# A four-layer network on one core: layer 0's gathers tied to its chain, layer 1's two branches in one stage, layer 3's attention written out

## The chip, the cores and the metric

The kernel runs on one core of one Trainium2 chip. The time is device microseconds of that core for one execution, and the median of the runs counts. Besides them one execution was recorded by the hardware profiler.

## What is computed

`x` is one sequence of 2048 tokens of 128 features, in float32. Each of four layers adds two branches that read the same normalised input; shortened from the reference:

```
xn = layernorm(x)
x = x + L0_attn(xn) + L0_ffn(xn)
xn = layernorm(x)
x = x + L1_attn(xn) + L1_ffn(xn)
xn = layernorm(x)
x = x + L2_attn(xn) + L2_ffn(xn)
xn = layernorm(x)
x = x + L3_attn(xn) + L3_ffn(xn)
```

- L0_attn is a recurrence over time: 16 heads of 8 features carry an 8x8 state, in each step `S = a*S + beta*(v - a*S k) k^T`, and put out `S q`. L0_ffn sends each token to the best 2 of 8 experts, `gelu(x W1a) * (x W1b) @ W2`, and adds the two results by weight.
- L1_attn is a linear attention, followed by its own residual, a second LayerNorm and a hidden MLP, `gelu(y @ W1 + b1) @ W2 + b2` with 512 hidden features.
- L1_ffn turns the 128 features into 64 units `s = xn @ Win + bin`. Each unit has a small net of its own with 16 inner neurons, `g = sum_j w2[u,j] * relu(w1[u,j]*s + b1[u,j]) + b2[u]`, and the branch gives `g @ Wout + bout`.
- L3_attn is causal attention with 16 heads of 64 features over 2048 tokens, in which `exp(s - max)` is divided by its masked sum; L3_ffn sends each token to the best of 8 experts.

## The kernel before

**Stages.** The program is a row of stages. The helper `stage` opens a block with one instruction stream for each engine and ends it with a barrier of all engines (L54 to L57); within a stage the engines wait for each other on counting semaphores (`wait_ge`, `then_inc`), and each stream runs in the order in which it is written. The features lie on the 128 partitions and the tokens along them, in NCH = 4 chunks of CH = 512 columns; `cs(c)` is chunk c. `x_features` is the residual x, `xn_features` the normalised input.

**Layer 0's join** is the end of the stage of `l0_recur`. The 2048 time steps are cut into NSEG = 64 segments of 32. The first part of the stage runs all segments at once; the join then carries the 8x8 states from one segment to the next, a chain of 64 steps. In step j TensorE multiplies a matrix of blocks with column block T[j] (L928) and raises `t_next`; VectorE waits for it, adds to get T[j+1] (L1093, 128x8) and raises `t_ready`, for which TensorE's next step waits. In the gaps TensorE does the parts of the experts that are still open and the products `carry` (L911), which VectorE adds up in blocks of 512 columns (L1080). Beside it POOL, once all expert rows are stored (`stored0`, `stored1`), issues 2*NT = 32 gathers in a plain loop, each an indirect DMA of 128 rows of 128 features (L813). They bring every token its two expert rows into `r_rows`, which the next stages read.

**Layer 1's tail** is three stages. `hidden_mlp`: for each chunk c TensorE does four products `mlp_up` (L1537), ScalarE four Gelus (L1552), TensorE four products that add up in `mlp_down` (L1542), VectorE one add onto x (L1565); POOL adds the attention's residual (L1558). Its weights come in the LayerNorm stage before, by SP's queue (`loads`, L255). Then `layer1_ffn` loads its 14 small tiles in a stage of their own (`load_all`, L309 on SP and L315 on ScalarE, seven each), and runs the units' stage. Two token halves share the 128 partitions: units of chunks 0 and 1 on partitions 0 to 63, those of chunks 2 and 3 on 64 to 127, so `units` is 128x1024. VectorE clears the unused corners of the weights, TensorE multiplies, ScalarE copies with a bias (L1738), then for each of two column halves 16 Relus of 128x512 with the neuron's weight and bias (L1744), each followed on VectorE by a multiply-and-add into `unit_out` (L1758, L1761). Four products with `w_out` (L1732) and four adds onto x (L1766) end the stage.

**Layer 3's attention** handles 16 heads, two and two in a pair. The function `heads` writes an engine's stream: a prologue, the first pair, a hardware loop `Fori` over pairs 1 to 6 (L2475), the last pair, an epilogue. Each engine runs a loop of its own, with a register as the counter from which the waits' values are worked out. A head's score products (L2676), its projections for the following head (L2656), exponentials (L2762), casts (L2777), transposes by DMA, and products with v (L2696) stand within it in an order that the program lays down by hand.

## Time and profile before

| | |
|---|---|
| median of 3 runs | 2175.07 us (2172.19 to 2177.26) |
| the profiled execution, its own time | 2190.24 us |
| its span in the trace | 2188.5 us |
| TensorE, busy with matmuls | 1770.6 us (81%) |
| TensorE, busy with weight loads | 1132.2 us (52%) |
| VectorE | 1416.3 us (65%) |
| ScalarE | 1231.0 us (56%) |
| POOL | 1133.9 us (52%) |

PE is TensorE's matmuls, PEld its weight loads, DVE is VectorE, ACT ScalarE, POOL GpSimd, SP the engine whose queue carries most plain transfers; a name with a q behind it is an engine's own sequencer. An arrow `out<-in` names the tiles; behind it stands their shape. Idle time in square brackets or behind a bar is that of the engine just before the instruction, with what ended it. The clock is TensorE's granted clock as a share of its full speed. All times count from the start of the span. Attention in layer 3 takes the stretch from 1190 to 2120 us, layer 1's tail that from 666 to 744, and the join of layer 0 ends at 574.

### The profile page before, as it was taken

To read this page: it belongs to the slowest core of one execution; us is meant where nothing else is said; L and a number is where in the kernel's file an instruction comes from. 1 tells how busy PE (TensorE), PEld (TensorE's weight loads), DVE (VectorE), ACT (ScalarE), POOL (GpSimd) and SP (SyncE) were. 2 spreads that over 40 slices of the span, in tenths; PEclk is the share of its full clock that TensorE was granted. 3 is DMA by queue.
4 is the path that set the end of the run, shared out by engine and by line. 5 is a ranking of instruction groups with operands and counts; after the bars stand their busy time and mean duration, and the time that the engine had idled before them with its cause. 6 is when DMAs were issued, how large, how long until landed. Compare 5 with 4: busy or idle time off the path is not lost. (4 is left out here: it accounts for less than half of the span.)

```text
span 2188.5 us, 33555 instructions
## 1 busy us (share of the span) xinstructions
PE 1770.6 (81%) x10687; PEld 1132.2 (52%) x10687; DVE 1416.3 (65%) x2100; ACT 1231.0 (56%) x2080; POOL 1133.9 (52%) x1025
## 2 busy tenths in 40 slices
PE   5637999995777457577887999989999999999968
PEld 2414777785643146463463455555555555555544
DVE  2475777761351668684416888878887878888831
ACT  3264333343243636433535877777777777777743
POOL 1053555425000066421113788878787878888860
PEclk7577999996688789898899999999999999999979
DMA  1212222221000000000411899999999999999970
GB/s 27 61 36 71 78 78 78 78 61 39 7 11 8 4 2 0 3 1 4 123 38 29 146 160 152 158 154 163 153 163 157 158 163 159 158 163 160 168 138 20
DMA packets 630959, 193.09 MB, mean 88 GB/s; under 512 B 591553, under 2 KB 622034, under 8 KB 630814
## 3 DMA queue, kind: packets, MB, share of 16 engines
q1 hardware_dynamic: 621062, 167.25, 43.5%
q0 software_dynamic: 8224, 23.51, 3.5%
q8 instruction: 95, 1.56, 0.3%
q10 hardware_dynamic: 1528, 0.37, 0.1%
q14 instruction: 50, 0.41, 0.1%
HBM read 36.90 MB, written 12.48 MB: 23 GB/s over the span
## 5 line engine op out<-in xcount | busy, mean ns | idle before, releaser
L2847 DVE TENSOR_REDUCE half_max<-scores 128x1 f32<-128x1024 f32 x512 | 613.9, 1219 | 127.0 <-PE scores L2676 119.6
L2593 POOL TENSOR_TENSOR p_low<-p,p_high 128x2048 f16<-128x2048 f32 (+15 forms) x256 | 576.2, 2251 | 147.4 <-ACT p_high L2777 134.5
L2762 ACT ACTIVATE p<-scores,exp_bias 128x1024 f32<-128x1024 f32 (+7 forms) x384 | 317.5, 861 | 82.2 <-DVE exp_bias L2852 80.6
L2676 PE MATMUL scores<-k_high,q_pair 128*128 128x512 f16 x1024 | 306.1, 380 | 69.5 <-ACT p L2762 51.7
L2777 ACT ACTIVATE p_high<-p 128x2048 f16<-128x2048 f32 (+15 forms) x256 | 282.5, 1104 | 41.3 <-DMA pT_high<-p_high 36.0
L2676 PE MATMUL scores<-k_low,q_pair 128*128 128x512 f16 x1024 | 305.8, 380 | 0.0
L2696 PEld LDWEIGHTS scores<-v_pair,pT_high 128*128 128x128 f16 x2176 | 152.3, 99 | 102.7 <-issue 68.5
L2696 PE MATMUL scores<-v_pair,pT_low 128*128 128x129 f16 x2176 | 186.4, 222 | 9.2 <-DMA pT_low<-p_low 9.1
L2696 PE MATMUL scores<-v_pair,pT_high 128*128 128x129 f16 x2176 | 188.7, 222 | 3.6 <-DMA pT_high<-p_high 2.9
L2696 PEld LDWEIGHTS scores<-v_pair,pT_low 128*128 128x128 f16 x2176 | 147.8, 99 | 43.3 <-DMA pT_low<-p_low 12.1
L2676 PEld LDWEIGHTS scores<-k_low,q_pair 128*128 128x128 f16 x1024 | 99.8, 97 | 122.8 <-issue 2.2
L2676 PEld LDWEIGHTS scores<-k_high,q_pair 128*128 128x128 f16 x1024 | 79.1, 97 | 124.8 <-ACT p L2762 51.6
L2587 POOL TENSOR_TENSOR p<-p,past 128x128 f32<-128x128 f32 x256 | 116.6, 456 | 37.8 <-ACT p L2762 36.5
L950 ACT ACTIVATE gelu_out<-expert_up,r_b 128x256 f32<-128x256 f32 x92 | 43.4, 472 | 146.1 <-PE expert_up L841 143.1
L841 PEld LDWEIGHTS expert_up<-slot_features,w_up 128*128 128x128 f32 x368 | 97.2, 321 | 46.1 <-DVE hidden L1030 26.0
L841 PE MATMUL expert_up<-slot_features,w_up 128*128 128x256 f32 x368 | 110.4, 424 | 12.1 <-DVE hidden L1030 11.0
L802 POOL TENSOR_TENSOR a_Z<-r_Z,r_a 128x512 f32<-128x512 f32 x31 | 55.2, 1782 | 115.5 <-DVE r_Z L1047 115.5
L2784 ACT ACTIVATE o_raw<-scores 128x258 f32<-128x258 f32 x128 | 49.4, 386 | 92.3 <-PE scores L2696 92.3
L2852 DVE TENSOR_SCALAR exp_bias<-half_max 128x1 f32<-128x1 f32 x256 | 54.9, 214 | 25.9
L2656 PE MATMUL scores<-xn_features,w_q 128*128 128x512 f32 x128 | 70.7, 638 | 0.0
L2656 PE MATMUL scores<-xn_features,w_k 128*128 128x512 f32 x128 | 69.9, 632 | 0.8 <-DVE k_low L2832 0.8
L1558 POOL TENSOR_TENSOR x_features<-x_features,x_res 128x512 f32<-128x512 f32 x4 | 4.9, 1258 | 116.2 <-SPq L54 116.2
(486 smaller groups left out, 3320.7 us busy)
## 6 DMA issues: line engine op xcount, KB each, us to landing
pT_high<-p_high SPq DMA_TRANSPOSE x256, 3.6
pT_low<-p_low SPq DMA_TRANSPOSE x256, 3.8
slots<-zero_row SPq DMA_DIRECT2D x1, 3036.0 KB, 14.4
slot_rows<-slots SPq DMA_DIRECT2D x23, 132.0 KB, 2.4
slots_out<-expert_out SPq DMA_DIRECT2D x23, 128.0 KB, 1.8
w_up<-in_L_ffn_inter_w_dram SPq DMA_DIRECT2D x1, 2048.0 KB
dispatched<-moe_rows SPq DMA_DIRECT2D x1, 1024.0 KB
slot_rows<-dispatched SPq DMA_DIRECT2D x4, 256.0 KB, 3.9
```

The costliest lines, as they stand in the source:

```text
L802: pool.tensor_tensor(aZ[:], Z[:, 0, :, :], wide(r.a[:, t + 1, :]), ALU.mult).then_inc(az_ready, 1)
L841: mm = pe.matmul(hps[:, n % 2, s, :], up_w[:, i % 4, s, f, :], xs[:, i % 2, :], start=True, stop=True)
L2587: pool.tensor_tensor(diag, diag, tri[:], ALU.mult).then_inc(masked, 1)
L2593: pool.tensor_tensor(flat(pl[:, buf, b0:b0 + n, :]), flat(p32[:, buf, b0:b0 + n, :]), flat(ph[:, buf, b0:b0 + n, :]), ALU.subtract).then_i ...
L2656: pe.matmul(ps[:, b, :], w[:, par, :, :].rearrange("p r d -> p (r d)"), m.xn[:, cs(c)], start=True, stop=True).then_inc(done, 1)
L2676: mm = pe.matmul(ps[:, b.start + i, :], q, k[:, par, cs(2 * half + i)], start=start, stop=not start)
L2696: mm = pe.matmul(o_pair[:, p % 2, 0:VW], (pTh, pTl)[part][:, buf, b0 + b, :], v2[:, par, b, 0:VW], start=(part == 0 and b == 0), stop=(par ...
L2762: act.activation(flat(p32[:, buf, b0 + first:b0 + first + w, :]), flat(ps[:, banks(p, half), :])[:, 0:w * P], ACT.Exp, bias=bias[:, p:p + ...
L2777: act.activation(flat(ph[:, buf, b0:b0 + n, :]), flat(p32[:, buf, b0:b0 + n, :]), ACT.Copy)\
L2784: act.activation(raw[:, par, 2 * pair:2 * pair + 2, :], o_pair[:, :, 0:VW], ACT.Copy).then_inc(o_out, 1)
L2847: dve.tensor_reduce(mx[:, p % 2, half:half + 1], flat(ps[:, b[half], :]), AX.X, ALU.max, negate=True)\
L2852: dve.tensor_scalar(bias[:, p:p + 1], mx[:, p % 2, 0:1], mx[:, p % 2, 1:2], math.log(LIFT), ALU.min, ALU.add).then_inc(biased, 1)
```

## The change

It has three parts.

**In `l0_recur`** each of the 32 gathers waits for a count of `t_ready`: gather i for NSEG - 2*NT - 2 + i = 30 + i steps of the chain.

```diff
--- before.py
+++ after.py
@@ -817,6 +817,7 @@
                 pool.wait_ge(stored0, 16 * ((TILES + 1) // 2))
                 pool.wait_ge(stored1, 16 * (TILES // 2))
                 for i in range(2 * NT):
+                    pool.wait_ge(t_ready, NSEG - 2 * NT - 2 + i)
                     gather(i)
```

**In layer 1** the MLP and the units' branch become one stage, `hidden_mlp_and_units`. The 14 small tiles join the two weights in SP's queue of the LayerNorm stage before, and the stage of loads is gone. The Relus and their sums run over 1024 columns, 16 of each, and ScalarE has one before each Gelu. VectorE puts the MLP's adds between the sums, the first three after the sums of neurons j = 6, 10 and 14, the fourth after the last. The four products with `w_out` use the memory of `mlp_up`.

```diff
@@ -1522,34 +1523,60 @@
-def hidden_mlp(nc, m, src, wa, wb, b1, b2, base):
+def hidden_mlp_and_units(nc, m, w, src, base):
+    FIRST = 3
...
+        s, inner, g = sb("units", [P, w.HALF]), sb("unit_hidden", [P, 4, w.HALF]), sb("unit_out", [P, w.HALF])
         ups, yps = own.enter_context(psum(nc, "mlp_up", [P, 4, CH])), own.enter_context(psum(nc, "mlp_down", [P, 2, CH]))
+        sps = own.enter_context(psum(nc, "units_in", [P, 2, CH]))
...
             @block.tensor
             def _(pe):
+                pe.wait_ge(cleared, 4)
+                for c in range(2):
+                    for h in range(2):
+                        mm = pe.matmul(sps[:, c, :], w.inp[:, h, :, :].rearrange("p a u -> p (a u)"), m.xn[:, cs(2 * h + c)],
+                                       start=(h == 0), stop=(h == 1))
+                    mm.then_inc(units_in, 1)
                 for c in range(NCH):
...
                     mm.then_inc(down, 1)
+                pe.wait_ge(summed, w.INNER)
+                for c in range(NCH):
+                    pe.matmul(ups[:, c, :], w.out[:, c // 2, :], g[:, cs(c % 2)], start=True, stop=True).then_inc(units_out, 1)
 
             @block.scalar
             def _(act):
+                def neuron(j):
+                    if j >= 4:
+                        act.wait_ge(summed, j - 3)
+                    act.activation(inner[:, j % 4, :], s[:], ACT.Relu, bias=w.b1[:, j:j + 1], scale=w.w1[:, j:j + 1])\
+                       .then_inc(relued, 1)
+
+                for c in range(2):
+                    act.wait_ge(units_in, c + 1)
+                    act.activation(s[:, cs(c)], sps[:, c, :], ACT.Identity, bias=w.ends[:, 0:1]).then_inc(units_ready, 1)
+                act.wait_ge(units_ready, 2)
                 for c in range(NCH):
                     if c >= 2:
                         act.wait_ge(down, c - 1)
                     for f in range(FT):
+                        neuron(c * FT + f)
                         act.wait_ge(up, c * FT + f + 1)
...
             @block.vector
             def _(dve):
-                for c in range(NCH):
+                def add(c):
                     dve.wait_ge(down, c + 1)
                     dve.wait_ge(based, c + 1)
...
+                for h in range(2):
+                    dve.memset(w.inp[:, h, 1 - h, :], 0.0).then_inc(cleared, 1)
+                    dve.memset(w.out[(1 - h) * w.U:(2 - h) * w.U, h, :], 0.0).then_inc(cleared, 1)
+                for j in range(w.INNER):
+                    dve.wait_ge(relued, j + 1)
...
+                        dve.wait_ge(summed, j)
+                        dve.scalar_tensor_tensor(out=g[:], in0=inner[:, j % 4, :], scalar=w.w2[:, j:j + 1], in1=g[:],
+                                                 op0=ALU.mult, op1=ALU.add).then_inc(summed, 1)
+                    if j % FT == FIRST - 1 and j > FT:
+                        add(j // FT - 1)
+                add(NCH - 1)
+                for c in range(NCH):
+                    dve.wait_ge(units_out, c + 1)
+                    dve.wait_ge(added, c + 1)
+                    dve.scalar_tensor_tensor(out=m.x[:, cs(c)], in0=ups[:, c, :], scalar=m.col("L1_ffn_bout"),
+                                             in1=m.x[:, cs(c)], op0=ALU.add, op1=ALU.add).then_inc(units_added, 1)
@@ -1692,81 +1739,22 @@
-        hidden_mlp(nc, m, y, wa, wb, "L1_attn_b1", "L1_attn_b2", xres)
-
-
-def layer1_ffn(nc, m, inp):
...
+                  loads=[(w.up[:], inp["L1_attn_W1"]), (w.down[:], inp["L1_attn_W2"].rearrange("(t p) n -> p t n", p=P))]
+                  + [(w.inp[:, h, h, :], inp["L1_ffn_Win"]) for h in range(2)]
+                  + [(w.out[half(h), h, :], inp["L1_ffn_Wout"]) for h in range(2)]
+                  + [(t[half(h)], inp[name]) for t, name in ((w.w1, "L1_ffn_W1"), (w.b1, "L1_ffn_b1"), (w.w2, "L1_ffn_W2"))
+                     for h in range(2)]
+                  + [(w.ends[half(h), i:i + 1], inp[name].rearrange("(m o) -> m o", o=1))
+                     for i, name in ((0, "L1_ffn_bin_"), (1, "L1_ffn_b2")) for h in range(2)])
+        hidden_mlp_and_units(nc, m, w, y, xres)
```

**In layer 3's attention** `heads` writes all eight pairs one behind the other, on every engine; there is no loop, and all waits have constant values. The order within a pair is the same.

```diff
@@ -2471,10 +2459,8 @@
-        pair(0, True, False)
-        with eng.Fori(1, H // 2 - 1) as i:
-            pair(i, False, False)
-        pair(H // 2 - 1, False, True)
+        for i in range(H // 2):
+            pair(i, i == 0, i == H // 2 - 1)
         epilogue(lambda per_head, k, ahead=0: H * per_head + ahead * per_head + k)
```

The order of the instructions shows the first two parts. Tiles have the program's names; a row with x15 stands for 15 like it; the names of semaphores in brackets are those of the stage that first used the number. POOL, end of the stage of `l0_recur`, before:

```order
L779 DMA w_up<-in_L_ffn_W_dram,r_wrow 128x1024 [waits down_1486]
L781 DMA w_down<-in_L_ffn_W_dram,r_wrow 128x512
L779 DMA w_up<-in_L_ffn_W_dram,r_wrow 128x1024 [waits down_1486]
L781 DMA w_down<-in_L_ffn_W_dram,r_wrow 128x512
L813 DMA r_rows<-slots_out,r_slot 128x128 [waits stored1_1489,stored0_1488]
L813 DMA r_rows<-slots_out,r_slot 128x128 x31
```

and now:

```order
L779 DMA w_up<-in_L_ffn_W_dram,r_wrow 128x1024 [waits down_1486]
L781 DMA w_down<-in_L_ffn_W_dram,r_wrow 128x512
L779 DMA w_up<-in_L_ffn_W_dram,r_wrow 128x1024 [waits down_1486]
L781 DMA w_down<-in_L_ffn_W_dram,r_wrow 128x512
L813 DMA r_rows<-slots_out,r_slot 128x128 [waits t_ready_1480,stored1_1489,stored0_1488]
L813 DMA r_rows<-slots_out,r_slot 128x128 [waits t_ready_1480] x31
```

Every gather has a wait on `t_ready` now; nothing else on POOL in this stage moved.

ScalarE, the stages of the MLP and of the units, before:

```order
L1552 ACT_TABLE_LOAD
L1552 ACTIVATE mlp_hidden<-mlp_up,cols 128x512 [waits rows_zeroed_63] x8
L1552 ACTIVATE mlp_hidden<-mlp_up,cols 128x512 [waits rows_zeroed_63,shaped_65]
L1552 ACTIVATE mlp_hidden<-mlp_up,cols 128x512 [waits rows_zeroed_63] x3
...
L1738 ACTIVATE units<-units_in,unit_biases 128x512 [waits ones_set_64]
L1744 ACTIVATE unit_hidden<-units,unit_b_6340,unit_w_6339 128x512 [waits shaped_65]
L1744 ACTIVATE unit_hidden<-units,unit_b_6340,unit_w_6339 128x512 x7
L1744 ACTIVATE unit_hidden<-units,unit_b_6340,unit_w_6339 128x512 [waits vectors_turned_67] x8
L1738 ACTIVATE units<-units_in,unit_biases 128x512 [waits ones_set_64]
```

and now the start of the merged stage:

```order
L1571 ACTIVATE units<-units_in,unit_biases 128x512 [waits x_loaded_69] x2
L1566 ACTIVATE unit_hidden<-units,unit_b_6096,unit_w_6095 128x1024 [waits picked_70]
L1579 ACT_TABLE_LOAD
L1579 ACTIVATE mlp_hidden<-mlp_up,cols 128x512 [waits ones_set_64]
L1566 ACTIVATE unit_hidden<-units,unit_b_6096,unit_w_6095 128x1024
L1579 ACTIVATE mlp_hidden<-mlp_up,cols 128x512 [waits ones_set_64]
L1566 ACTIVATE unit_hidden<-units,unit_b_6096,unit_w_6095 128x1024
L1579 ACTIVATE mlp_hidden<-mlp_up,cols 128x512 [waits ones_set_64]
L1566 ACTIVATE unit_hidden<-units,unit_b_6096,unit_w_6095 128x1024
L1579 ACTIVATE mlp_hidden<-mlp_up,cols 128x512 [waits ones_set_64]
L1566 ACTIVATE unit_hidden<-units,unit_b_6096,unit_w_6095 128x1024 [waits activated_250]
```

The two copies of the units stand first, the load of the Gelu's table stands behind the first Relu, and Relus of 1024 columns and Gelus alternate, where all 16 Gelus stood ahead of all 32 Relus.

VectorE, the same stages, before:

```order
L1565 SCALAR_TENSOR_TENSOR x_features<-mlp_down,cols,x_features 128x512 [waits rows_loaded_66,shaped_65] x4
...
L1758 TENSOR_SCALAR unit_out<-unit_hidden,unit_w_6341,unit_biases 128x512 [waits rows_loaded_66]
L1761 SCALAR_TENSOR_TENSOR unit_out<-unit_hidden,unit_w_6341,unit_out 128x512 [waits vectors_turned_67,rows_loaded_66] x15
L1758 TENSOR_SCALAR unit_out<-unit_hidden,unit_w_6341,unit_biases 128x512 [waits rows_loaded_66]
L1761 SCALAR_TENSOR_TENSOR unit_out<-unit_hidden,unit_w_6341,unit_out 128x512 [waits vectors_turned_67,rows_loaded_66] x15
L1766 SCALAR_TENSOR_TENSOR x_features<-units_out,cols,x_features 128x512 [waits cols_ready_68] x4
```

and now, behind the four clearings of w_in and w_out:

```order
L1601 TENSOR_SCALAR unit_out<-unit_hidden,unit_w_6097,unit_biases 128x1024 [waits scaled_249]
L1604 SCALAR_TENSOR_TENSOR unit_out<-unit_hidden,unit_w_6097,unit_out 128x1024 [waits activated_250,scaled_249] x6
L1592 SCALAR_TENSOR_TENSOR x_features<-mlp_down,cols,x_features 128x512 [waits vectors_turned_67,rows_loaded_66]
L1604 SCALAR_TENSOR_TENSOR unit_out<-unit_hidden,unit_w_6097,unit_out 128x1024 [waits activated_250,scaled_249] x4
L1592 SCALAR_TENSOR_TENSOR x_features<-mlp_down,cols,x_features 128x512 [waits vectors_turned_67,rows_loaded_66]
L1604 SCALAR_TENSOR_TENSOR unit_out<-unit_hidden,unit_w_6097,unit_out 128x1024 [waits activated_250,scaled_249] x4
L1592 SCALAR_TENSOR_TENSOR x_features<-mlp_down,cols,x_features 128x512 [waits vectors_turned_67,rows_loaded_66]
L1604 SCALAR_TENSOR_TENSOR unit_out<-unit_hidden,unit_w_6097,unit_out 128x1024 [waits activated_250,scaled_249]
L1592 SCALAR_TENSOR_TENSOR x_features<-mlp_down,cols,x_features 128x512 [waits vectors_turned_67,rows_loaded_66]
L1612 SCALAR_TENSOR_TENSOR x_features<-mlp_up,cols,x_features 128x512 [waits cols_ready_68,loaded_251] x4
```

The MLP's adds (L1592, before L1565) stand between the sums, and the 30 sums and 2 first products of 512 columns became 15 and 1 of 1024.

## Rows read from the trace of the kernel before

**Rows 1.** Timeline of VectorE, layer 0's join (start, us, instruction, idle time before it).

```profile
515.11 0.17 DVE L1093 TENSOR_TENSOR T<-u_product,r_Z 128x8 f32<-128x8 f32 x1 [0.75 <-PE u_product L928]
...
553.66 0.17 DVE L1093 TENSOR_TENSOR T<-u_product,r_Z 128x8 f32<-128x8 f32 x1 [10.36 <-remote]
554.51 0.17 DVE L1093 TENSOR_TENSOR T<-u_product,r_Z 128x8 f32<-128x8 f32 x1 [0.69 <-PE u_product L928]
...
566.66 0.17 DVE L1093 TENSOR_TENSOR T<-u_product,r_Z 128x8 f32<-128x8 f32 x1 [0.69 <-PE u_product L928]
...
573.65 0.69 DVE L1080 TENSOR_TENSOR xn_features<-q_sums,r_wo 128x512 f32<-128x512 f32 x1 [6.22 <-PE q_sums L911]
```

**Rows 2.** Adds of tile T from 509 on, and VectorE's waits (sum, number, longest).

```profile
L1093 DVE TENSOR_TENSOR T<-u_product,r_Z x31: 166/167/168, 509.0 to 566.7; 128x8 f32<-128x8 f32 x31
...
DVE T L1093 <- remote: 35.2, 7, 10.4
```

**Rows 3.** POOL's gathers and drain, by line (shortest/median/longest ns, first to last start).

```profile
L813 POOLq MOVE  x32: 29/29/29, 508.2 to 533.4; - x32
L813 POOL DMA_INDIRECT r_rows<-slots_out,r_slot x32: 992/997/999, 509.0 to 549.3; - x32
...
L54 POOLq DRAIN  x1: 22016/22016/22016, 534.7 to 534.7; - x1
```

**Rows 4.** Windows: stretch, us, busy PE, PEld, DVE, ACT, POOL, clock, DMA share, GB/s.

```profile
654.40:666.50 12.10, 7.10 (x16) 2.96 (x16) 7.67 (x13) 8.63 (x13) 0.00 (x0) 0.90 0.15 45
666.50:698.20 31.70, 29.91 (x64) 12.90 (x64) 3.00 (x4) 12.28 (x17) 4.93 (x4) 0.93 0.00 0
698.20:706.20 8.00, 0.00 (x0) 0.00 (x0) 0.04 (x1) 0.00 (x0) 0.00 (x0) 0.72 0.13 21
706.20:744.30 38.10, 13.54 (x16) 4.72 (x16) 26.85 (x40) 24.04 (x34) 0.00 (x0) 0.61 0.00 0
```

**Rows 5.** Groups by form, 660 to 745 (busy us, mean ns, idle before).

```profile
L1744 ACT ACTIVATE unit_hidden<-units,unit_b,unit_w 128x512 f32<-128x512 f32 x32 | 22.8, 799 | 0.1
L1761 DVE SCALAR_TENSOR_TENSOR unit_out<-unit_hidden,unit_w,unit_out 128x512 f32<-128x512 f32 x30 | 22.5, 751 | 3.2 <-ACT unit_hidden L1744 0.2
...
L1552 ACT ACTIVATE mlp_hidden<-mlp_up,cols 128x512 f32<-128x512 f32 x16 | 11.0, 687 | 15.0 <-PE mlp_up L1537 14.8
```

**Rows 6.** Timeline of layer 1's tail (two records of TensorE are one matmul).

```profile
666.55 5.88 PE L1537 MATMUL mlp_up<-l_y,w_up 128*128 128x512 f32 x8 [5.00 <-PEq L57]
...
679.13 3.60 PE L1542 MATMUL mlp_down<-mlp_hidden,w_down 128*128 128x512 f32 x8
...
701.82 0.60 SPq L309 DMA_DIRECT2D unit_biases<-in_L_ffn_b_dram  x1
...
742.87 0.75 DVE L1766 SCALAR_TENSOR_TENSOR x_features<-units_out,cols,x_features 128x512 f32<-128x512 f32 x1 [0.94 <-PE units_out L1732]
...
744.33 1.28 ACT L269 ACT_TABLE_LOAD   x1 [9.51 <-PEq L57]
```

**Rows 7.** ScalarE's casts in layer 3, groups by form, 1190 to 2120.

```profile
L2777 ACT ACTIVATE p_high<-p 128x2048 f16<-128x2048 f32 x16 | 30.6, 1910 | 30.3 <-DMA pT_high<-p_high 30.3
...
L2777 ACT ACTIVATE p_high<-p 128x1024 f16<-128x1024 f32 x16 | 16.8, 1048 | 2.0 <-DMA pT_high<-p_high 2.0
```

**Rows 8.** Layer 3: TensorE's waits, its branch, two windows, two projections.

```profile
PE scores L2676 <- issue: 14.7, 7, 3.2
...
L2475 PEldq COMPARE_BRANCH  x6: 79/4003/4238, 1426.4 to 2002.1; - x6
...
1432.20:1548.00 115.80, 105.80 (x834) 61.47 (x833) 95.03 (x117) 89.48 (x121) 93.89 (x72) 1.00 0.96 159
1892.60:2006.30 113.70, 105.71 (x834) 61.28 (x833) 95.32 (x117) 89.19 (x121) 92.60 (x71) 1.00 0.96 159
...
1314.87 1.02 PE L2656 MATMUL scores<-xn_features,w_k 128*128 128x512 f32 x2
...
2006.29 1.02 PE L2656 MATMUL scores<-xn_features,w_k 128*128 128x512 f32 x2
```

92 lines of the change are left out of this document (20 added, 72 removed).

## The prediction

> **What bounds the kernel now.** The kernel is a row of stages with a barrier between them, and a stage lasts as long as its slowest engine, so I read three stretches one by one and ask in each what ends last; the shares over the whole span say nothing on them. The order was: the timeline of VectorE in layer 0's join, what it waited for, POOL's queue there, the windows of layer 1, its groups by form and its timeline, and last what TensorE waited for in layer 3.
>
> Layer 0's join: a chain of 64 steps, each a tiny matmul on TensorE and a 128x8 add on VectorE. 31 of the adds lie from 509.0 on, so the one at 509.0 is step 34 [rows 2], 515.11 is step 41 and 553.66 step 49 [rows 1]. Left alone, a step takes 0.85 us (553.66 to 554.51, or 15 steps from 553.66 to 566.66 with 13.0 us). From 515.11 to 553.66 eight steps took 38.6 us; seven of them waited 35.2 us in all, the longest 10.4, for a signal that the trace can't put down to an engine ("remote") [rows 2]. Just then POOL issues 32 gathers, one per 1.30 us, from 509.0 to 549.3; its sequencer has the last in its queue at 533.4, and its drain at the end of the stage starts at 534.7 and lasts 22.0 us, so POOL counts as finished only at 556.7 [rows 3]. The first five gathers fell beside steps of usual length: the disturbance starts some 6 us into the gathers and grows.
>
> Layer 1's tail: the MLP takes 31.7 us, a stage of loads 8.0, the units' stage 38.1, 77.8 in all from 666.5 to 744.3 [rows 4]. In the MLP TensorE is busy 29.9 of 31.7 us and bounds; in the units' stage VectorE (26.9) and ScalarE (24.0) share the work, and TensorE does 13.5 us.
>
> Layer 3: six pairs of heads ran as a loop. TensorE's branch back took 4.0 us at the median of six, 79 ns where it was not taken; TensorE stood idle 14.7 us before the scores with nothing that the trace can name [rows 8]. A pair keeps TensorE busy 105.8 us of 115.8, and the DMA share is 0.96 [rows 8]: two resources stand close behind any bubble.
>
> **Part A, the join.** Removed: nothing. Added: one wait on a count of steps before each of the 32 gathers, gather i for step 30 + i. Nothing but gathers and the drain stands behind these waits on POOL, and no gathered row is read before the next stage. Do the waits bind? At 509.0 step 34 is done, so gathers 0 to 4 may go, and an unhindered chain frees one per 0.85 us while POOL takes 1.30: they would not delay POOL at all. But each wait stands before the gather is queued, so POOL's sequencer no longer runs ahead: at 515.1 it could have queued gather 11, from then on one per step. If it is the deep queue that holds the chain's signals up, this regulates itself: a slow chain feeds POOL less. That is my choice, because the delays begin some gathers in and not with the first. Then the chain ends no later than POOL: 515.11 + 23 steps x 0.85 = 534.7, its tail to the last add 574.3 - 566.7 = 7.7 us more [rows 1], 542.4. POOL's end, 556.7, becomes the stage's end in place of 574.3: **17.6 us gained**. The cost of a wait itself no row shows; its bounds are nothing and one step of 0.85 for each gather once (a gather that comes a step late), and I take nothing, since POOL is the slower of the two. The gain's bounds: 24.0 if POOL is done 1.0 us after the last gather's start (549.3 + 1.0 = 550.3), and below nothing, see the rivals.
>
> The Trainium skill (SBUF — State Buffer, § Who interferes with whom) states that VectorE and GpSimd contend only for one shared pair of ports, and that a VectorE instruction with at most one SBUF input outside the 2-port modes does not take part. The chain's add reads one operand from PSUM and one from SBUF, so by that page gathers can't hold it up and the waits have nothing to cure; the five undisturbed steps agree, the seven delays of up to 10.4 us do not. What A would be by it is the first rival.
>
> **Part B, layer 1's tail in one stage.** The stage of loads goes (8.0 us) and its 14 transfers move to SP's queue in the LayerNorm stage before, behind two others. A transfer of this kind takes SP 0.60 us of issue [rows 6], all 16 some 9.0; from the end of the last issue shown (702.4) to the next stage's start (706.2) 3.8 us passed. That makes 12.8 us beside a LayerNorm stage of 12.1 [rows 4], 0.7 too much; I take 0.4 us lost, between that and nothing.
> ScalarE now does 16 Relu over 1024 columns in place of 32 over 512, each ahead of a Gelu. At 512 it takes 799 ns [rows 5]; another 512 columns cost (1910 - 1048)/2 = 431 ns [rows 7], so 1.23 us, with the Gelu's 0.69 and some 0.18 of overlap between neighbours 1.74 us a pair. (From above: twice 799 less overlap, 1.42 us.) VectorE's 16 sums cost at most twice the 0.75 us of a sum over 512 [rows 5], 1.5 us, and stay below ScalarE's pace.
> The sum from the stage's start: four matmuls on a slow start, as the MLP's first four, 5.9 [rows 6]; the clearing before them 0.7 and the second copy of units with its hand-overs 1.0, both my estimates (a copy over 512 columns is an activation as the Relu's 0.8); 7.6. First group of four pairs 4 x 1.74, and the Gelu table load, which now stands behind the first Relu and no longer under TensorE's start, 1.28 [rows 6]: 8.2. In the other three groups the first Gelu waits for TensorE: four matmuls take 3.6 us [rows 6], so after a group's last Gelu one "down" and one "up", 0.9 each, with hand-overs 2.1, then the Gelu's 0.69 and three pairs: 8.0 each, 24.0. Tail: last down 0.9, four output matmuls 3.6, one add 0.75: 5.2. The barrier to the next LayerNorm 0.7 (742.87 + 0.75 to 744.33) [rows 6]. Together 45.7 us for 77.8, less the 0.4: **31.7 us gained** (27 with the dear Relu, 35 if TensorE starts at full clock).
>
> **Part C, layer 3 written out.** From the first projection of the loop's first pair (1314.87) to that of the last pair after it (2006.29) are 691.4 us for six pairs [rows 8]. The last of them, with no jump behind it, took 113.7 (1892.6 to 2006.3) [rows 8]; six such would be 682.2: **9.2 us gained**. Bounds: 0, if the transposes (DMA share 0.96) hold the pace, and 14.7, all of TensorE's unnamed idle time. What the longer code costs no row shows; its bounds are nothing and the 2.0 us by which the jumping pairs were slower, and I take nothing, since the pairs at either end were already written out.
>
> **Sum.** 17.6 + 31.7 + 9.2 = 58.5 us against the profiled execution's own 2190.2 (its span is 2188.5), which gives 2131.7. The median of the runs, 2175.1, lies 15.2 below that execution; I take the same 58.5 from it: **2116.6 us**. A part of the 15.2 may itself be delays in the join that unprofiled runs don't have; that speaks for less gain, and the range leans that way.
>
> **Rivals.**
> 1. The join stays as it is (28%). The waits bind only from about gather 16, when the long delays have begun; what holds the signal up is a gather in flight, not a deep queue. For: the longest delay (10.4 us, before 553.66) came when POOL's sequencer had long stopped queueing. Against: the first five gathers. A = 0: 2175.1 - 40.9 = 2134.2. The Trainium skill's rule above gives this same time.
> 2. TensorE falls to 1.2 GHz in the merged stage (6%). It has gaps there now; in the units' stage the granted clock averaged 0.61, in the MLP 0.93 [rows 4]. At half clock the 32 matmuls of the MLP take 1.8 us each, 28 us more: B = 4, 2144.
> 3. Layer 3's pace is the transposes' (7%): C = 0, 2125.8.
> 4. Slower than before (3%): tying POOL to the chain spreads the gathers, so that each of the last 23 steps meets one, where now the last 15 run free of them. These 23 took 51.6 us (515.11 to 566.66). With B and C at 40.9 it turns slower when the join loses 45.3 us more, which is from 4.2 us a step; the eight disturbed steps took 4.8 us each [rows 1]. At 4.8 for all 23 the join takes 59 us more: 2134.2 + 58.8 = 2193. Against it: one gather per step is little beside the 10.4 us wait, in which POOL could issue eight.
> That a part doesn't do what it says is rival 1 for A and 3 for C.
>
> **How the numbers follow.** My case 56%, rivals 28, 6, 7 and 3%. The range runs from A and C at their upper bounds with B near its sum (2175.1 - 24 - 35 - 14.7 = 2101) to rival 1 with B and C a little below theirs, 2138; it leaves out rivals 2 and 4 and the far ends. About 0.2% (4.4 us) is what a measurement of this kernel can tell from no change. Faster in all cases but the fourth and what lies between: 0.96; same 0.01; slower 0.03.
>
> **What would show it.** A: no add of the chain waits over 2 us, the last add lies before POOL's end, the stage ends some 17 us earlier. B: from the merged stage's start to the next LayerNorm 45 us, Relu of 1024 columns 1.23 us, ScalarE the busiest engine. C: no branch on TensorE, pairs of 113.7 us. Wrong it would be with a granted clock of 0.5 in the merged stage, delays in the join as before, or pairs still at 115.

## The result and the profile after

| | before | changed |
|---|---|---|
| median of the runs | 2173.63 us (2168.95 to 2177.26, 4 runs) | 2139.66 us (2138.41 to 2141.9, 4 runs) |
| the profiled execution, its own time | 2190.24 us | 2138.84 us |
| its span | 2188.5 us | 2135.9 us |

The ratio is 0.9851, 95% interval [0.9835, 0.9868]: 34 us faster where 58.5 were forecast, and 2139.7 lies outside the range that ended at 2138. The two profiled executions differ by 51.4 us, though. The execution before was 16.6 us slower than this median of its kernel (15.2 above that of the three runs before), the changed one was within 0.9 us of its own.

A stage's length can be read from POOL's first instruction behind the barrier at its end and that of the stage before. These three stretches carry the change (us):

| stretch | before | changed | forecast gain | gain in the traces |
|---|---|---|---|---|
| layer 0's stage with the join | 394.2 | 376.1 | 17.6 | 18.1 |
| layer 1's tail | 77.9 | 45.2 | 31.7 | 32.7 |
| layer 3's attention | 977.6 | 977.5 | 9.2 | 0.1 |

So by the traces alone two parts came out to a microsecond, and one not at all. The median agrees with neither the sum of the forecasts nor that of the traces.

**The join.** VectorE's timeline in the changed kernel, the same stretch as [rows 1]:

```profile
515.10 0.17 DVE L1094 TENSOR_TENSOR T<-u_product,r_Z 128x8 f32<-128x8 f32 x1 [0.69 <-PE u_product L929]
...
529.87 0.17 DVE L1094 TENSOR_TENSOR T<-u_product,r_Z 128x8 f32<-128x8 f32 x1 [0.69 <-PE u_product L929]
...
536.86 0.69 DVE L1081 TENSOR_TENSOR xn_features<-q_sums,r_wo 128x512 f32<-128x512 f32 x1 [6.22 <-PE q_sums L912]
```

POOL's gathers and its drains up to 600 us, answering to [rows 3], and VectorE's waits in the chain (sum, number, longest):

```profile
L813 POOLq MOVE  x32: 29/29/29, 503.2 to 528.4; - x32
L813 POOL DMA_INDIRECT r_rows<-slots_out,r_slot x32: 992/997/1000, 504.0 to 544.3; - x32
...
L54 POOLq DRAIN  x5: 34/34/22024, 529.7 to 587.2; - x5
```

```profile
DVE T L1094 <- PE u_product L929: 19.0, 27, 0.8
```

No add waited over 0.8 us, the last lies at 529.9, and POOL's drain, 529.7 + 22.0 = 551.7, ends the stage, 47.7 us after the first gather as before (556.7 - 509.0).

**Layer 1's tail.** The window of the merged stage, its groups by form, ScalarE's table load, and the products of one chunk with the start of the next, answering to [rows 4, 5]:

```profile
644.60:690.30 45.70, 38.77 (x80) 14.88 (x80) 26.06 (x28) 30.51 (x35) 4.92 (x4) 0.95 0.00 1
```

```profile
L1566 ACT ACTIVATE unit_hidden<-units,unit_b,unit_w 128x1024 f32<-128x1024 f32 x16 | 19.8, 1237 | 0.0
L1604 DVE SCALAR_TENSOR_TENSOR unit_out<-unit_hidden,unit_w,unit_out 128x1024 f32<-128x1024 f32 x15 | 19.2, 1282 | 9.8 <-ACT unit_hidden L1566 9.8
...
L1579 ACT ACTIVATE mlp_hidden<-mlp_up,cols 128x512 f32<-128x512 f32 x16 | 10.9, 682 | 2.8 <-PE mlp_up L1550 2.8
```

```profile
653.38 1.28 ACT L1579 ACT_TABLE_LOAD   x1
```

```profile
669.38 3.60 PE L1550 MATMUL mlp_up<-l_y,w_up 128*128 128x512 f32 x8
672.81 2.90 PE L1555 MATMUL mlp_down<-mlp_hidden,w_down 128*128 128x512 f32 x6
676.30 1.13 PE L1555 MATMUL mlp_down<-mlp_hidden,w_down 128*128 128x512 f32 x2 [0.58 <-ACT mlp_hidden L1579]
677.26 3.60 PE L1550 MATMUL mlp_up<-l_y,w_up 128*128 128x512 f32 x8
```

The Relu over 1024 columns takes 1.237 us (1.23 forecast), and the clock is granted at 0.95 of full speed. ScalarE was not the busiest engine, as had been forecast: TensorE was busy 38.8 of 45.7 us, ScalarE 30.5. In a group of 7.9 us ScalarE waits some 0.9 us for TensorE's first product, and TensorE 0.6 us for the last Gelu, so the two take turns.

**Layer 3.** What TensorE waited for from 1137 to 2072 in the changed kernel (time in us, times, longest), and a window of one pair, answering to [rows 8]:

```profile
PE scores L2662 <- ACT p L2748: 63.1, 88, 2.2
PE scores L2682 <- DMA pT_low<-p_low: 14.6, 20, 2.0
PE scores L2682 <- DMA pT_high<-p_high: 8.4, 11, 1.9
```

```profile
1375.46:1490.04 114.58, 104.33 (x833) 61.36 (x832) 95.27 (x117) 89.00 (x120) 94.09 (x73) 1.00 0.95 160
```

The 14.7 us of unnamed idle time are gone, and so is the branch. But the waits for the transposes rose from 12.0 to 23.0 us and those for ScalarE from 51.7 to 63.1. The pair shown takes 114.6; the six middle pairs take 114.9 on average, where they took 115.2 before. Before, in a window of the same length, the same waits were:

```profile
PE scores L2676 <- ACT p L2762: 51.7, 83, 2.2
PE scores L2696 <- DMA pT_low<-p_low: 9.1, 10, 2.7
PE scores L2696 <- DMA pT_high<-p_high: 2.9, 4, 1.2
```

Two questions are left for the chip. Is the join's gain there in runs that nobody records? And why did layer 3 give next to nothing?

### The profile page after: what moved, and what is told of

It reads as the page before. It is cut to its first block and busy times, and to the rows that moved or that the text cites. A ratio compares the mean times of both kernels' runs of the same rounds, so it can differ in the third digit from the quotient of the medians.

```text
span 2135.9 us, 31634 instructions
## 1 busy us (share of the span) xinstructions
PE 1751.4 (82%) x10687; PEld 1129.4 (53%) x10687; DVE 1415.0 (66%) x2084; ACT 1224.6 (57%) x2064; POOL 1135.8 (53%) x1025
## 5 line engine op out<-in xcount | busy, mean ns | idle before, releaser
L2662 PE MATMUL scores<-k_high,q_pair 128*128 128x512 f16 x1024 | 304.1, 378 | 68.1 <-ACT p L2748 63.1
L2682 PE MATMUL scores<-v_pair,pT_low 128*128 128x129 f16 x2176 | 187.3, 223 | 15.2 <-DMA pT_low<-p_low 14.6
L802 POOL TENSOR_TENSOR a_Z<-r_Z,r_a 128x512 f32<-128x512 f32 x31 | 56.3, 1815 | 114.9 <-DVE r_Z L1048 114.9
L2642 PE MATMUL scores<-xn_features,w_k 128*128 128x512 f32 x128 | 65.3, 596 | 0.6 <-DVE k_low L2818 0.6
L862 PE MATMUL q_sums<-Z_q,sum_pick 128*128 128x128 f32 x512 | 62.4, 275 | 0.0
L813 POOL DMA_INDIRECT r_rows<-slots_out,r_slot x32 | 31.9, 996 | 57.0 <-DVE T L1094 48.7
```

What stands on the lines that cost most here:

```text
L802: pool.tensor_tensor(aZ[:], Z[:, 0, :, :], wide(r.a[:, t + 1, :]), ALU.mult).then_inc(az_ready, 1)
L862: mm = pe.matmul(qs[:, 0:P], m.sum_pick[:, d, :], Zq[:, b % 2, k, d, :, :], start=(d == 0), stop=(d == HD - 1))
L2642: pe.matmul(ps[:, b, :], w[:, par, :, :].rearrange("p r d -> p (r d)"), m.xn[:, cs(c)], start=True, stop=True).then_inc(done, 1)
L2662: mm = pe.matmul(ps[:, b.start + i, :], q, k[:, par, cs(2 * half + i)], start=start, stop=not start)
L2682: mm = pe.matmul(o_pair[:, p % 2, 0:VW], (pTh, pTl)[part][:, buf, b0 + b, :], v2[:, par, b, 0:VW], start=(part == 0 and b == 0), stop=(par ...
```

## The experiments

The stretches of all profiled executions, read as above (us; "join" is layer 0's stage with the join). The kernel before was run beside each group of experiments, with medians from 2169.29 to 2173.63 where it had more than one run, so times of two kernels are best compared by their ratios to it:

| kernel | join | layer 1's tail | layer 3's attention | median |
|---|---|---|---|---|
| before (for comparison) | 394.2 | 77.9 | 977.6 | 2173.63 |
| before again | 376.7 | 77.8 | 978.4 | one run, 2176.85 |
| waits alone | 376.6 | 77.8 | 975.0 | 2167.65 |
| merged tail alone | 376.4 | 45.2 | 979.5 | 2142.83 |
| layer 3 written out alone | 376.7 | 77.7 | 971.7 | 2169.83 |
| before, half the gathers | 362.6 | 77.6 | 978.3 | 2157.41 |
| changed | 376.1 | 45.2 | 977.5 | 2139.66 |
| changed, extra products | 376.5 | 45.2 | 990.7 | 2156.28 |
| changed, narrow products | 376.6 | 45.2 | 980.2 | 2143.45 |
| changed, half transposes | 376.5 | 45.2 | 935.0 | 2100.14 |
| the same in the loop | 376.7 | 44.9 | 953.2 | 2120.35 |
| half transposes, narrow products | 376.7 | 45.2 | 933.0 | 2098.84 |
| changed, split gathers | 365.7 | 45.2 | 977.2 | 2126.7 |
| the same, table first | 365.6 | 43.7 | 973.9 | 2123.3 |

### The three parts, each alone

**The waits alone**, on the kernel before:

```diff
                 for i in range(2 * NT):
+                    pool.wait_ge(t_ready, NSEG - 2 * NT - 2 + i)
                     gather(i)
```

> The kernel before with the waits of the 32 gathers alone. Theory R: the delays of the chain are found only in an execution that the profiler records; in the plain runs the chain ends before POOL's drain, which ends the stage with or without the waits. Then the median stays within 0.2% of before, while the profiled execution is some 18 us shorter than the one of before (about 2172) and its join ends at some 48 us after the first gather. Theory W: the delays are there in every run and the waits remove them; the median falls by 12 to 18 us, and something else lost as much in the whole change.

Measured: 2167.65 against 2170.47 us of the kernel before on the same chip, ratio 0.999, interval [0.9972, 1.0008]. By the ratio that is 2.2 us of gain, give or take 3.9, so the waits are worth next to nothing in plain runs. Theory W falls. Of theory R the half on plain runs holds. The profiled execution had no delays, as both theories wanted.

**The merged tail alone**: the diff of layer 1 as in the change, with layer 3's loop and without the waits.

> Layer 1's merged stage alone. Both theories: the two traces show 77.9 us of stages turned into 45.2, so the median falls by 32 to 33 us (2141). If only some 15 to 20 us come, the clock or the loads behave otherwise in plain runs than in the profiled one. The profiled execution: by theory R it has the delays in the join again (an add of the chain that waited over 5 us) and lies about 15 us above its own median.

Measured: 2142.83 against 2170.47, ratio 0.9865 [0.9841, 0.9889], which is 29.3 us less by the ratio (24 to 35) and 27.6 by the medians. The stretch itself went from 77.8 to 45.2 in the trace. But the second half of the expectation failed: this kernel has no waits before its gathers, it was recorded by the profiler, and its join took 376.4 us with no delay. So theory R was wrong on its other half too: being recorded is not what brings the delays.

**Layer 3 written out, alone**: the change's edit of `heads` on the kernel before.

> Layer 3's attention written out, alone. Theory T: the pace there is held by the ring of casts, transposes and products; the branch's 4 us only stood in a gap that opens elsewhere once it is gone. The median within 0.2% of before. Rival: the jumps cost 9 us (2165) and in the whole change something else lost them. By T the time that TensorE waited for nothing named (14.7 us) goes to zero and its waits for the transposes rise from 11 to 22 us.

Measured: 2169.83, ratio 0.9994 [0.9979, 1.0009]: 1.3 us of gain, give or take 3.3. Theory T's number, and its waits too: the unnamed idle time went to zero and the waits for transposes to 22.5 us. But in the profiled execution the six middle pairs took what the prediction had said, 681.5 us in all for its 682.2, from 113.2 to 114.0 each. The last two of them:

```profile
1692.04:1805.83 113.79, 104.50 (x834) 61.52 (x832) 95.28 (x117) 89.13 (x120) 93.93 (x73) 1.00 0.94 160
1805.83:1919.05 113.22, 104.57 (x833) 61.55 (x832) 95.27 (x117) 89.12 (x120) 94.08 (x73) 1.00 0.92 158
```

The stage took 971.7 us there, and the same code 977.5, 977.2 and 973.9 in other profiled executions, while the loop took from 975.0 to 979.5 in five. The means are 975.1 and 977.8, with overlap. So the gain of writing it out is not shown to be nothing. It is at most some 5 us, by the interval of the plain runs (1.3 + 3.3), which leaves out the 9.2 that were forecast.

This kernel's join also ran without waits and undisturbed. Its gathers, and what VectorE waited for in the chain from 505 to 567 us:

```profile
L813 POOLq MOVE  x32: 29/29/29, 503.4 to 528.6; - x32
L813 POOL DMA_INDIRECT r_rows<-slots_out,r_slot x32: 992/997/999, 504.2 to 544.5; - x32
```

```profile
DVE T L1093 <- PE u_product L928: 19.7, 28, 0.8
```

Without any wait POOL's sequencer ran through its moves from 503.4 to 528.6, with the waits of the changed kernel from 503.2 to 528.4. An add was never held for more than 0.8 us in either. The waits hardly change when POOL queues its gathers: at 503.2 the undisturbed chain had done step 33, so the first four gathers were free at once, and from there it frees one per 0.85 us, while the sequencer, left to itself, takes one per 0.81. Both are faster than POOL with one gather per 1.30 us, so the queue is as deep with the waits as without.

### The kernel before, recorded once more

No edit.

> The kernel before once more, nothing edited, for its profile. If the delays of the join belong to this kernel under the profiler (and to the exact code that the two runs without waits in their joins did not have), they are here again: adds of the chain waiting over 5 us, a stage of 394 us, a profiled time of some 2190. If they were an event of that one execution, the stage takes 376 us as in the runs with layer 1's merged stage alone and with layer 3 alone, and the time is 2165 to 2180.

Measured: 2176.85 us, its join 376.7 us. VectorE's waits in the join, and POOL's gathers:

```profile
DVE T L1093 <- PE u_product L928: 20.3, 29, 0.8
```

```profile
L813 POOLq MOVE  x32: 29/29/29, 511.8 to 537.0; - x32
L813 POOL DMA_INDIRECT r_rows<-slots_out,r_slot x32: 992/997/999, 512.6 to 552.9; - x32
```

The same instructions, the same 32 gathers, no "remote" wait. The 35.2 us of [rows 2] were an event of that one execution. Five profiled executions had no waits before the gathers, and one of them showed it. No plain run of the kernel before, of more than forty, came above 2181.14 us, while that execution took 2190.24. What the event was stays open: it did not come again, so no experiment could show its cause, or whether the waits would have kept it short.

### Who ends the join

On the kernel before; every token's second expert row is left out:

```diff
-                for i in range(2 * NT):
+                for i in range(NT):
                     gather(i)
...
-                pe.wait_ge(r.gathered, 16 * 2 * NT)
+                pe.wait_ge(r.gathered, 16 * NT)
```

> The kernel before with only the first 16 gathers, so every token's second expert row is left out (the products over them still run, on other data). Who ends the join in plain runs? If POOL's 32 gathers and the drain behind them (theory R), half of them gone bring its end from 556.7 to below the chain's own end of 542: 14 to 15 us faster. If the chain with its delays ends the stage (theory W), the gain is what half the gathers take off the delays: the last add moves from 566.7 towards 535, 18 to 30 us faster. If neither, no change.

Measured: 2157.41, ratio 0.9936 [0.9914, 0.9959], 13.9 us less by the ratio (13.1 by the medians), and 14.1 us less in the stage of the trace (376.7 to 362.6). That is theory R's number. The gathers, POOL's part of the barrier and its drain, and the chain's last add into `xn_features`:

```profile
L813 POOLq MOVE  x16: 29/29/29, 504.3 to 512.0; - x16
L813 POOL DMA_INDIRECT r_rows<-slots_out,r_slot x16: 993/997/1001, 505.0 to 524.6; - x16
```

```profile
L54 POOLq EVENT_SEMAPHORE  x6: 17/17/17, 538.9 to 559.8; - x6
...
L54 POOLq DRAIN  x3: 34/34/18159, 512.5 to 542.2; - x3
```

```profile
538.08 0.69 DVE L1080 TENSOR_TENSOR xn_features<-q_sums,r_wo 128x512 f32<-128x512 f32 x1 [6.22 <-PE q_sums L911]
```

POOL is done at 512.5 + 18.2 = 530.7, and the barrier falls at 538.9, right behind the end of the chain's own last add (538.8). So in plain runs it is POOL's work and drain that end the join, with and without the waits. The chain has 14 us of slack: in the changed kernel it ends at 537.6 and POOL at 551.7. That is why a repair of the chain could bring nothing.

### What sets layer 3's pace

**Extra products** on TensorE, where the branch stood, on the changed kernel:

```diff
-                    def project(at, par, u, b):
+                    def project(at, par, u, b, again=0):
...
-                        pe.matmul(ps[:, b, :], w[:, par, :, :].rearrange("p r d -> p (r d)"), m.xn[:, cs(c)],
-                                  start=True, stop=True).then_inc(done, 1)
+                        for _ in range(again + 1):
+                            mm = pe.matmul(ps[:, b, :], w[:, par, :, :].rearrange("p r d -> p (r d)"), m.xn[:, cs(c)],
+                                           start=True, stop=True)
+                        mm.then_inc(done, 1)
...
-                                        project(at, 1 - par, s, UBANK)
+                                        project(at, 1 - par, s, UBANK, again=4 if s == 0 and par == 0 else 0)
```

> The changed kernel, with the first projection of every second head in layer 3 made five times in place of once (same operands, same result): 4 x 0.86 = 3.4 us more of TensorE per pair at the place where the branch stood, 8 of them, 27 us more in all. Theory T (TensorE has slack there, the pace is set by the ring of cast, transposes and products): the time rises by under 8 us, and TensorE's waits for the transposes and for ScalarE fall by about what was added. Theory P (TensorE sets the pace, and the 4 us branches really stood in it): the time rises by 20 to 27 us.

Measured: 2156.28, ratio 0.9941 [0.9919, 0.9962], 16.6 us more than the changed kernel by the medians, 20 by the ratios (0.9941 - 0.9851 of 2171, give or take 6), and 13.2 in the stage of one execution each. The medians and the stage are neither theory's number, and the ratios reach the lower edge of theory P's. So between a half and three quarters of the 27 us came through by these figures. At this place TensorE has some cover, but not one of 3.4 us in each pair.

**Narrow products**, on the changed kernel; three quarters of all queries' and keys' columns are left out:

```diff
-                        pe.matmul(ps[:, b, :], w[:, par, :, :].rearrange("p r d -> p (r d)"), m.xn[:, cs(c)],
+                        few = slice(c * CH, c * CH + CH // 4)
+                        pe.matmul(ps[:, b, 0:CH // 4], w[:, par, :, :].rearrange("p r d -> p (r d)"), m.xn[:, few],
                                   start=True, stop=True).then_inc(done, 1)
```

> The changed kernel, with layer 3's projections cut to 128 of their 512 columns (three quarters of queries and keys are left out; all later steps run on what stands in the buffers). TensorE has some 8 x 0.64 us less per head, 10 us per pair, 82 us in all. Theory T: the time falls by under 25 us, and TensorE's idle time takes the rest. Theory P: it falls by 60 to 82 us.

Measured: 2143.45, ratio 0.9882 [0.9855, 0.9909], where the changed kernel had 2139.66 and 0.9851; no gain (7 us more by the ratios, give or take 7). Its waits from 1139 to 2075:

```profile
PE scores L2663 <- ACT p L2749: 126.0, 120, 3.2
PE scores L2683 <- DMA pT_high<-p_high: 15.7, 24, 1.9
```

TensorE's busy time fell from 840.4 to 773.9 us, and its wait for ScalarE's exponentials rose from 63.1 to 126.0. What is taken off TensorE it waits out elsewhere. Theory P, that TensorE's own work sets the pace, falls.

**Half transposes**, on the changed kernel; the second half of each transpose is left out, and the products run over the first half twice:

```diff
+                        n = (n + 1) // 2
                         sp.dma_start_transpose(pTh[:, buf, b0:b0 + n, :], flat(ph[:, buf, b0:b0 + n, :]))
...
+                        n = (n + 1) // 2
                         sp.dma_start_transpose(pTl[:, buf, b0:b0 + n, :], flat(pl[:, buf, b0:b0 + n, :]))
...
-                            mm = pe.matmul(o_pair[:, p % 2, 0:VW], (pTh, pTl)[part][:, buf, b0 + b, :], v2[:, par, b, 0:VW],
+                            mm = pe.matmul(o_pair[:, p % 2, 0:VW], (pTh, pTl)[part][:, buf, b0 + b % ((n + 1) // 2), :], v2[:, par, b, 0:VW],
```

> The changed kernel, with each transpose of layer 3 cut to the first half of its blocks (the other half of the probabilities is left out; the products run over the first half twice). The DMA share falls from 0.93 to about 0.5. Theory T in its form that the transposes set the pace: the stage of 977 us falls by over 60 us. Theory T in its form that it is the latency of the whole ring: 10 to 60 us. If neither, TensorE with its 105 of 115 us sets it: under 10 us.

Measured: 2100.14, ratio 0.9683 [0.9661, 0.9705], 39.5 us less than the changed kernel by the medians, 36.5 by the ratios, and 42.5 in the stage. Two pairs of it:

```profile
1262.60:1372.20 109.60, 103.70 (x834) 61.50 (x833) 95.29 (x117) 89.09 (x121) 94.00 (x73) 1.00 0.52 90
1372.20:1481.80 109.60, 103.71 (x833) 61.53 (x832) 95.29 (x117) 89.10 (x121) 93.99 (x73) 1.00 0.55 90
```

All six middle pairs take 109.6 us, where with full transposes they scatter from 113.9 to 116.6 in the changed kernel. The DMA share falls from between 0.90 and 0.95 to between 0.52 and 0.56. So about 5 us of every pair, and the scatter, come from full transposes. A stage shorter by 42.5 us is in the band of the theory that a transpose's length counts as one step of a ring (10 to 60 us), and not in that of transposes that set the pace alone (over 60). Something else then holds 109.6.

**The same in the loop**: the kernel with half transposes, with the three lines of the loop over pairs 1 to 6 put back.

> As the run with half transposes (the second half of each transpose is left out, the products run over the first half twice), but with layer 3's pairs in the hardware loop again. There each of the six written-out pairs took 109.6 us to the tenth. Theory T (the branch's 4 us stand in time that the full transposes take from the ring anyway): with short transposes the branches show, and each looping pair takes 111 to 113.6 us; the stage 7 to 20 us longer than the 935.0 of the straight form, the median 2107 to 2120. Rival (a branch is hidden whatever the transposes do, since the other engines run ahead over it): pairs of 109.6 again, within 3 us of 2100.

Measured: 2120.35, ratio 0.9775 [0.9746, 0.9804]: 20 us more than written out, 18.2 in the stage. TensorE's unnamed idle time from 1137 to 2047, its branch, that of VectorE, and a pair:

```profile
PE scores L2666 <- issue: 11.4, 5, 2.5
```

```profile
L2463 PEldq COMPARE_BRANCH  x6: 79/3675/3917, 1368.3 to 1933.1; - x6
...
L2463 DVEq COMPARE_BRANCH  x6: 50/56/72, 1370.7 to 1935.5; - x6
```

```profile
1363.90:1476.60 112.70, 105.61 (x828) 61.57 (x827) 93.95 (x115) 88.04 (x119) 93.69 (x72) 0.98 0.51 87
```

This is the run that settles it. With short transposes the five taken branches cost 18 us, 3.6 each, which is all that the branch itself takes (3.4 to 3.9). With full ones the loop costs at most some 5 us more than the written-out form. The branch was a real cost, and most of it was hidden beneath the waits for the transposes. Only TensorE pays it: on VectorE the same branch, also taken five times, takes 0.07 us at most.

**Both cuts** in the changed kernel, half transposes and narrow products:

> The changed kernel with both cuts in layer 3: transposes over half their blocks and projections over a quarter of their columns (all that is left out as before). Narrow projections alone gave nothing, short transposes alone 42 us of the stage. Theory T2 (two resources side by side, transposes first and TensorE right behind): with both cuts the stage falls by 42 and a good part of the 82 us that TensorE saves, 60 to 110 in all, 2030 to 2080. Theory R2 (with short transposes the ring of ScalarE, VectorE and POOL sets 109.6, TensorE has slack): nothing on top of the 42, 2095 to 2105.

Measured: 2098.84, ratio 0.9678 [0.9649, 0.9707], the stage 933.0: 2.0 us below half transposes alone. The longest waits from 1137 to 2033, of TensorE, ScalarE's exponentials and VectorE:

```profile
PE scores L2665 <- ACT p L2751: 120.2, 143, 2.2
```

```profile
ACT p L2751 <- DVE exp_bias L2841: 84.4, 144, 3.6
```

```profile
DVE half_max L2836 <- PE scores L2665: 111.3, 145, 2.0
```

Theory R2's number. The amount of TensorE's work is not the next limit, though it was busy 103.7 of 109.6 us with half transposes alone. It waits for the exponentials `p`, ScalarE for `exp_bias`, VectorE for the scores. Read from these waits, a loop of scores, maxima and exponentials over three engines sets the 109.6, and none of the three is full. It would also explain why a late start on TensorE costs time and less work on it gives none. No run shows this loop to be the limit: none of its three links was shortened.

### A version that is faster than both

Built on the changed kernel. Since POOL ends the join, eight of the 32 gathers can go where POOL idles: into the stage of `l0_output`, whose products over gathered rows come late. The gathers go in the order of the tokens, so that TensorE can start on the first 24, and the load of `w_o` moves into the stage, which saves the stage of that load.

```diff
-                for i in range(2 * NT):
+                for i in range(EARLY):
                     pool.wait_ge(t_ready, NSEG - 2 * NT - 2 + i)
                     gather(i)
...
-        load_all(nc, [(wo[:], inp["L0_attn_Wo"])])
...
+            @block.sync
+            def _(sp):
+                sp.dma_start(wo[:], inp["L0_attn_Wo"]).then_inc(wo_loaded, 16)
+
+            @block.gpsimd
+            def _(pool):
+                for i in range(EARLY, 2 * NT):
+                    gather_rows(pool, r, i).then_inc(late, 16)
...
-                pe.wait_ge(r.gathered, 16 * 2 * NT)
+                pe.wait_ge(r.gathered, 16 * EARLY)
                 for n in range(NT):
+                    if n == EARLY // 2:
+                        pe.wait_ge(late, 16 * (2 * NT - EARLY))
```

(EARLY is 24; `gather_rows` is the gather of before with the table column of token tile i // 2 and choice i % 2.)

> The changed kernel with the gathers in the order of the tokens, 24 of them in layer 0's join and 8 in the next stage with work, where POOL is idle, and with the load of w_o moved into that stage (one stage less). If POOL's gathers and its drain end the join in plain runs, as the run with half the gathers says, the join ends 10 us earlier and the small stage's 3 us go, but the last products over gathered rows still wait for POOL: 8 to 12 us faster than the changed kernel, 2128 to 2132. If the join's end is not POOL's, 3 us.

Measured: 2126.7 us (2124.1 to 2128.98), ratio to the kernel before 0.9797 [0.9781, 0.9814], where the change alone had 0.9851 [0.9835, 0.9868]: about 12 us faster than the changed kernel (give or take 5; 13.0 by the medians), a little more than expected. From the timeline of all engines:

```profile
538.05 0.69 DVE L1090 TENSOR_TENSOR xn_features<-q_sums,r_wo 128x512 f32<-128x512 f32 x1 [6.22 <-PE q_sums L921]
542.59 0.36 SPq L1125 DMA_DIRECT2D w_o<-in_L_attn_Wo_dram  x1
...
543.30 0.99 POOL L718 DMA_INDIRECT r_rows<-slots_out,r_slot  x1 [7.41 <-SPq L54]
...
545.43 8.24 PE L1149 MATMUL out_proj<-ident,r_rows 128*128 128x128 f32 x48
```

The next stage begins at 542, where in the changed kernel the stage of the load begins at 552, and the first 48 products over rows run while POOL gathers the rest. From the start of the join's stage to the end of `l0_output` it is 365.7 + 20.4 = 386.1 us, and 376.1 + 2.9 + 18.0 = 397.0 in the changed kernel. 2.9 of the 10.9 us are the stage of the load.

**The table first**, on top of that, in layer 1's merged stage:

```diff
+                act.preload_act_table_set("gelu_apprx_tanh_and_others")
                 for c in range(2):
                     act.wait_ge(units_in, c + 1)
```

> The kernel with split gathers, and in layer 1's merged stage the table of the Gelu loaded by ScalarE before the two copies of the units, while TensorE does its first products, in place of behind the first Relu. The load of 1.28 us leaves ScalarE's path: 1.3 us less, 45.2 to 43.9 for the stage, which the median (2126.7 before it) hardly shows; if the copies come later by it or the Relu loads a table of its own, nothing or worse.

Measured: 2123.3 us (2120.19 to 2126.67), ratio to before 0.9781 [0.9759, 0.9802]. ScalarE at the start of the stage:

```profile
637.35 1.28 ACT L1589 ACT_TABLE_LOAD   x1 [2.04 <-PEq L57]
641.95 0.69 ACT L1592 ACTIVATE units<-units_in,unit_biases 128x512 f32<-128x512 f32 x1 [3.32 <-PE units_in L1563]
```

The load stands in ScalarE's wait for TensorE, and the stage went from 45.2 to 43.7 us. The intervals of the two ratios overlap, so the medians do not tell these two kernels apart.

## Why the prediction was wrong, step by step

**Part A, the join: the step that failed is the choice of the cause.** I read one disturbed stretch in one execution as a property of the kernel, and counted 17.6 us for its repair. The arithmetic held in the traces (18.1), since it compared that stretch with an undisturbed one. But the waits did not bring it. The merged tail alone, layer 3 alone and the kernel before itself recorded again have no waits and took 376 to 377 us as well, and the chain of the run with half the gathers was undisturbed too. In plain runs the waits are worth 2.2 us, give or take 3.9. Two sentences of that part were wrong in their own right. "POOL's sequencer no longer runs ahead" is one: it queues at the same pace with and without the waits. The five gathers beside undisturbed steps, taken as evidence for a deep queue, are the other: in four executions without waits the queue was filled at the same pace and no step was held up, so its depth alone is not the cause. What I had in hand against the whole part was the 15.2 us by which the profiled execution stood above the median. I named it as a part that "may itself be delays in the join", and then took the full 58.5 from the median all the same. The 28% of rival 1 were too few for it.

The Trainium skill (SBUF — State Buffer, § Who interferes with whom) states that a VectorE instruction with at most one SBUF input outside the 2-port modes does not contend with GpSimd, and the chain's add is one. Every undisturbed execution agrees: 0.8 us was the longest wait of an add beside the gathers. Rival 1 named the right amount, a gain of about nothing, by luck: its ground was a gather in flight that holds the signal up, and the chain was not held up by 32 of them.

One step of A was right and became the useful one: POOL's drain is next to end the stage. Half the gathers took 14.1 us off the stage. The split of the gathers, with the load's stage gone, made 10.9 us of it in the traces.

**Part B, the merged tail: right but for the busiest engine.** 45.7 us were forecast for the stage and its barrier, 45.2 came. The Relu over 1024 columns took 1.237 us for 1.23, the later groups 7.9 us each for 8.0 (the products `mlp_up` of the last three chunks begin at 661.50, 669.38 and 677.26), the loads cost nothing in the LayerNorm stage (12.1 us before and after, where 0.4 were allowed). Alone it moved the median by 29.3 us (24 to 35), so the term holds there too. Rival 2 did not come: the granted clock was 0.95. The sign "ScalarE the busiest engine" was wrong: TensorE was busy 38.8 us, ScalarE 30.5. The sum had TensorE's products at the end of each group, so the time came out all the same.

**Part C, layer 3: the step that failed is reading the difference between pairs as the price of the branch.** The last pair, "with no jump behind it", took 113.7, and "six such would be 682.2". In the changed kernel, six pairs without any jump took 689.2 us (1261.53 to 1950.74), from 113.9 to 116.6 each. Layer 3 alone took 681.5 for them in its profiled execution, which the plain runs do not bear out as a gain. One pair of 113.7 was a draw from a scatter of 3 us that goes away with short transposes. The five branches cost 3.6 us each when the transposes are short, 18.2 in all and more than my upper bound of 14.7, and 1.3 us in all, give or take 3.3, when they are full. So the term of 9.2 us was too large: the time that the branch takes was for the most part hidden beneath the waits for transposes and exponentials, which rose when it went. The lower bound, "0, if the transposes (DMA share 0.96) hold the pace", was near the truth, and I gave it 7%. The DMA share of 0.96 beside TensorE's 105.8 of 115.8 should have weighed more. It said that a bubble on TensorE had company.

The Trainium skill (Runtime: NRT & Kernel Launch, § Instruction fetch mechanics) says that a taken branch to code outside the sequencer's window has to wait for a fetch, a reason to write loops out in full. The trace agrees that such a branch can stall: on TensorE 4.0 us taken and 79 ns not taken [rows 8], while the taken branches of the other engines' shorter streams took 45 to 72 ns. That the 4.0 us are a fetch no row here shows. What writing out paid depended on what stood beside it: 18 us under short transposes, and nothing that can be told from zero under full ones.

**The sum.** 29.3 (B), 2.2 (A) and 1.3 (C) make 32.8 us, give or take some 7, and the ratio of the change makes 32.4 (28.7 to 35.9). Of the 26.1 us that are missing to 58.5, A makes 15.4, C 7.9 and B 2.4 by these ratios. Rivals 1 and 3 both held nearly, at once, a case which I had not worked out: 2175.1 - 31.7 = 2143.4, 4 us from the result. The range stopped at one rival at a time.

## What to carry to other kernels

When the profiled execution is slower than the median of the runs by more than their scatter, find the stretch that it lost first, and do not count the repair of it as a gain until a second recording shows it again. An idle gap on the busiest engine is worth its length only if nothing else stands behind it: ask what else is nearly full (here the DMA share of 0.96) and could take its place, and take the scatter between equal repetitions as the smallest difference that a single repetition can show. To learn whether a cost is hidden, shorten what hides it, as the half transposes did for the branch.

## What the runs showed of the hardware that was not expected

- One execution of fourteen that were recorded lost some 18 us in a chain of tiny steps across TensorE and VectorE, with waits of up to 10.4 us that the trace can't put down to an engine. It did not come again.
- POOL's end comes well after its last gather: the last of 32 starts at 544.3 and takes 1.0 us, the drain ends at 551.7, 6.4 us later. With 24, 16 and 8 gathers in the stage (split gathers, half the gathers, and the stage of `l0_output` with split gathers) it ended 5.8, 5.1 and 2.0 us after the last. These stages with gathers at their end pay that.
- A taken branch back cost TensorE 3.8 to 4.2 us in the kernel before and 3.4 to 3.9 in the loop with half transposes. The same branch cost VectorE, ScalarE and POOL 0.045 to 0.072 us.
- Extra TensorE work at one place in layer 3 costs half of its length or more (13.2 of 27 us by the stage, 16.6 by the medians), while taking 66 us of TensorE's busy time away gives nothing that the runs show.
- With half the transposes, 12 heads in a row kept step to a tenth of a microsecond (109.6 us per pair); with full ones the pairs of the changed kernel scattered by 3 us (113.9 to 116.6) with the same instructions on TensorE.
